# End columns of the image strips as bf16 halves read in place, four masked key copies, full-tile values, and block results copied by ScalarE

## The reference, cut to what matters

```python
# tokens: depthwise 3x3 convolution, + bias, mean over 8x8 blocks        -> 64 tokens x 128
# layer 1: attention inside an image (softmax of q k^T), residual,
#          8 experts, top 2, plus 2 shared experts (128 -> 512 -> 128, gelu)
# layer 2: 8 heads of 16 channels, rotary position on q and k;
k_c = x_c @ wk_c.T            # 15 compressed keys and values: windows of 8 tokens,
v_c = x_c @ wv_c.T            # stride 4, weighted by a softmax of 8 gate logits
win_scores  = einsum(q, k) / 4      # 64 keys, causal, window 128
comp_scores = einsum(q, k_c) / 4    # 15 compressed keys, causal
# one softmax over 64 + 15 keys and a sink; then wo, residual, and a small
# MLP over the 128 channels with lower triangular weights
```

## Time and profile before

| what | value |
|---|---|
| time, median of 3 runs | 2063.84 us (2058.97 to 2075.73) |
| the profiled execution's own time | 2071.78 us |
| its span, first to last instruction | 2070.0 us |
| busy share: PE, DVE, ACT, POOL | 84%, 61%, 46%, 46% |
| mean granted TensorE clock | 0.925 of full speed |

### The profile page before, as it was taken

One profiled execution on the slowest core, in us unless ns is written; L12 is line 12 of the kernel. 1 busy time (PEld: TensorE's weight loads), 2 busy tenths in 40 slices (PEclk: granted clock), 3 DMA queues, 4 the chain that ended last, 5 costly groups with the idle time before them and its releaser, 6 DMA issues.

```text
span 2070.0 us, 47437 instructions
## 1 busy us (share of the span) xinstructions
PE 1745.7 (84%) x15216; PEld 1352.3 (65%) x15216; DVE 1268.4 (61%) x3484; ACT 948.9 (46%) x2291; POOL 950.9 (46%) x770
## 2 busy tenths in 40 slices
PE   1454879989897989899897989899897989998956
PEld 1443766868676776768676776768675776866644
DVE  2566456757675766767575766767675756753432
ACT  0122534546463645456363635445463635553522
POOL 1224245454556555464456464464445554533222
PEclk9999988989999999999898989999998989999986
DMA  6647454544544444545445444544445444301000
GB/s 245 243 163 255 179 201 167 194 154 152 203 183 168 181 168 175 199 148 192 157 178 204 181 155 155 211 158 172 165 168 209 179 136 170 131 20 50 17 26 6
DMA packets 109170, 332.08 MB, mean 160 GB/s; under 512 B 13662, under 2 KB 87585, under 8 KB 92412
## 3 DMA queue, kind: packets, MB, share of 16 engines
q1 hardware_dynamic: 86416, 300.90, 39.5%
q0 software_dynamic: 8992, 19.42, 2.9%
q10 hardware_dynamic: 13516, 8.51, 1.4%
HBM read 299.48 MB, written 29.29 MB: 159 GB/s over the span
## 4 chain that ended last, share of the span: by engine, by line
PE 65%; POOL 10%; issue 9%; DMA 7%; DVE 4%; ACT 2%; ACTq 1%; SPq 1%; POOLq 0%; DVEq 0%
PE hid_bank L598 11%; PE pool_bank L452 6%; DMA outs_d<-ys 5%; PE pool_bank L457 5%; POOL yg L1357 5%; PE sec_bank L654 4%; PE hid_bank L583 4%; PE sec_bank L674 4%; PE hid_bank L582 3%; PE sec_bank L665 3%; POOL xbuf L1346 3%; PE hid_bank L584 2%; PE sec_bank L617 2%; PE sec_bank L634 2%; PE down_bank L543 2%
## 5 line engine op out<-in xcount | busy, mean ns | idle before, releaser
L1346 POOL TENSOR_TENSOR xbuf<-xbuf 128x512 f32<-128x512 f32 x256 | 330.1, 1289 | 528.3 <-DVE xbuf L1039 518.5
L850 ACT ACTIVATE hid<-hid_bank,bias_t 128x128 f32<-128x128 f32 x960 | 273.7, 371 | 122.3 <-PE hid_bank L584 116.4
L598 PE MATMUL hid_bank<-w_s,hid 128*128 x1920 | 291.3, 297 | 0.0
L598 PEld LDWEIGHTS hid_bank<-w_s,hid 128*128 128x128 f32 x1920 | 243.8, 199 | 16.7
L1039 DVE TENSOR_TENSOR xbuf<-xbuf 128x1536 f32<-128x1536 f32 x128 | 236.7, 1849 | 25.9 <-DMA xbuf<-in_x 25.9
L582 PE MATMUL hid_bank<-xt,w_b 128*128 128x128 bf16 x960 | 201.3, 230 | 33.8 <-issue 18.4
L1060 DVE SCALAR_TENSOR_TENSOR taps<-pooled_s,tapw,taps 128x256 f32<-128x256 f32 (+1 forms) x416 | 210.0, 505 | 29.9 <-issue 21.6
L1043 DVE TENSOR_TENSOR xbuf<-xbuf 128x512 bf16<-128x512 f32 x128 | 90.3, 706 | 213.5 <-ACT xbuf L764 213.4
L1384 POOL TENSOR_TENSOR keys_h<-keys,heads 128x632 f32<-128x632 f32 x128 | 198.6, 1578 | 18.1 <-PE sec_bank L654 15.6
L1200 DVE COPY ys<-hid_bank 128x128 f32<-128x128 f32 x240 | 68.8, 287 | 219.0 <-PE hid_bank L598 192.8
L583 PE MATMUL hid_bank<-xt,w_b 128*128 128x128 bf16 x960 | 202.9, 230 | 0.1
(11 more groups left out here) (213 smaller groups left out, 3443.7 us busy)
## 6 DMA issues: line engine op xcount, KB each, us to landing
xbuf<-in_x SPq DMA_DIRECT2D x128, 2048.0 KB
rows_s<-rows_d SPq DMA_DIRECT2D x48, 320.0 KB, 8.9
outs_d<-ys SPq DMA_DIRECT2D x240, 64.0 KB
out<-h ACTq DMA_DIRECT2D x16, 256.0 KB
w_s<-in_w ACTq DMA_DIRECT2D x1, 2560.0 KB
hid<-in_w POOLq DMA_DIRECT2D x10, 256.0 KB, 3.7
rows_d<-x2r,spot_i POOLq DMA_INDIRECT x128
yg<-outs_d,spot_i POOLq DMA_INDIRECT x128
```

The source lines that it names most:

```text
L598: mm = nc.tensor.matmul(hid_bank[n % 2][:, 0:P], hid[:, n % RING, q * P:(q + 1) * P], w_q, start=False, stop=q == FC - 1)
L850: ins = nc.scalar.activation(hid[:, n % RING, cols], hid_bank[n % 2][:, cols], ACT.Gelu, bias=bias_t[:, q, j:j + 1])
L1346: nc.gpsimd.tensor_tensor(v[:, :, 1, :], v[:, :, 1, :], v[:, :, 2 * k + 3, :], ALU.add) \
```

## The change

- **End columns.** `halves` is laid over the fp32 data itself: channel c of a column is two bf16, h = 1 its upper 16 bits and h = 0 its lower 16. A new VectorE piece `ends` takes columns 0 and 7 of a buffer in one instruction (128 x 1024 elements), subtracts the upper half from the fp32 value and writes the rest, as bf16, into the lower half. The inner sum is split the same way in column 1, so ScalarE's `inner` is gone. The end columns are then pooled by pairs of bf16 matmuls with `block_b`. All these stationary operands now lie in memory with a step of two bf16 elements, where the inner sum's was contiguous.
- **Keys.** `keys_h` holds four copies (r = 0..3) of all keys of a group; copy r keeps the channels of heads r and r+4. ScalarE makes them with a scale per partition: four `Copy` instructions of 128 x 512 (`split`) and four of 128 x 120 (`pre.5`). A score matmul takes 64 of the 128 channels (rows 0:64 or 64:128). GpSimd's eight masking instructions are gone; `roped` has a tile of its own.
- **Values.** Four fp32 matmuls with 128 token columns, two images each, and two with 128 padded compressed columns (`xc` padded to 2 x 16 for an image, cleared once). ScalarE copies them with 2 instructions of 64 x 512 and 4 of 15 x 256.
- **Block results.** `narrow`'s copy to `ys` moves from VectorE to ScalarE.
- `sb2_b` keeps one copy of the row, read four times; `before_s` shares memory; all five lists of `ORDER` are new.

```diff
 ORDER sp:
-        store.9' load.0.0 store.11' load.0.1 store.12' store.10' store.13' store.14' rows.0 rows.1 load.1.0
+        store.8' store.6' store.10' store.7' store.11' store.12' load.0.0 store.9' load.0.1 store.13' store.14'
 ORDER pe:
-        up.0 up.1 table up.2 down.0 up.3 down.1 up.4 up.5 down.2 out' up.6 down.3 down.4 pool.0.0 pool.0.1
-        pool.0.2 up.7 down.5 down.6 att.1 down.7 att.2 lift.0 pool.0.3 lift.1 widen.0 widen.1 lift.2 att.3
+        up.0 up.1 table up.2 up.3 down.0 down.1 up.4 out' up.5 down.2 up.6 up.7 down.3 down.4 down.5 pool.0.0
+        pool.0.1 down.6 pool.0.2 down.7 att.1 lift.0 lift.1 widen.0 lift.2 att.2 widen.1 att.3 lift.3 pool.0.3
...
+        pool.3.1 lift.14 narrow.11 narrow.12 widen.13 widen.14 pool.3.2 narrow.13 pool.3.3 narrow.14 post.3
 ORDER act:
-        hidden.0 table hidden.1 hidden.2 hidden.3 hidden.4 inner.0.0 hidden.5 out' hidden.6 inner.0.1 hidden.7
+        hidden.0 hidden.1 table hidden.2 hidden.3 hidden.4 out' hidden.5 hidden.6 hidden.7 lift.0 att.1 lift.1
 ORDER dve:
-        tap.1.8' pair.0.0 tap.1.9' tap.1.10' tap.1.11' tap.1.12' tap.1.13' tap.1.14' inner.0.0 pair.0.1 att.0
+        tap.1.10' tap.1.11' tap.1.12' tap.1.13' tap.1.14' pair.0.0 ends.0.0 pair.0.1 att.0 inner.0.0 ends.0.1
 ORDER pool:
-        scatter.7' gather.0 gather.1 gather.2 gather.3 add.0.0 gather.4 add.0.1 gather.5 gather.6 gather.7
-        add.0.2 add.0.3 att.0 pre.1 add.1.0 add.1.1 pre.3 pre.4 pre.6 add.1.2 add.1.3 pre.7 score.2 score.4
+        scatter.6' scatter.7' gather.0 gather.1 gather.2 gather.3 gather.4 gather.5 gather.6 add.0.0 gather.7
+        add.0.1 add.0.2 att.0 add.0.3 pre.1 add.1.0 add.1.1 pre.3 pre.4 add.1.2 add.1.3 add.2.0 add.2.1 add.2.2
...
-        halves = [b[:].bitcast(bf16).rearrange("p (b x) (h c) -> p b x h c", x=8, h=2) for b in xbuf]
+        halves = [b[:].bitcast(bf16).rearrange("p (b x) (c h) -> p b x h c", x=8, h=2) for b in xbuf]
...
 PE, pool:
                     if k in (0, 2):
-                        eng.wait_ge(x_in[v], at(x_in[v], g, 16 * (u + 1)))
+                        eng.wait_ge(ends_low, at(ends_low, g, 2 * u + v + 1))
...
-                                nc.tensor.matmul(view[:, 0, :, side[bx]], halves[v][:, bx, 4, h, :], block_b[:],
+                                nc.tensor.matmul(view[:, 0, :, side[bx]], halves[v][:, bx, 1, h, :], block_b[:],
                                                  start=h == 0, stop=h == 1)
                         for bx in range(BX // 2):
-                            mm = nc.tensor.matmul(view[:, 1, :, side[bx]], blocks[v][:, bx, 0, :], block_sum[:],
-                                                  start=True, stop=True)
+                            for h in range(2):
+                                mm = nc.tensor.matmul(view[:, 1, :, side[bx]], halves[v][:, bx, 0, h, :], block_b[:],
+                                                      start=h == 0, stop=h == 1)
...
 PE, values:
-                    for m in range(4):
-                        im = 4 * half + m
-                        nc.tensor.matmul(bank[0:L, m * C:(m + 1) * C], x3t[:, im * L:(im + 1) * L], second["v"][:],
-                                         start=True, stop=True)
-                        mm = nc.tensor.matmul(bank[L:LK, m * C:(m + 1) * C], xc[:, im, :], second["vc"][:],
-                                              start=True, stop=True)
+                        for t in range(T):
+                            mm = nc.tensor.matmul(b1[:, t * C:(t + 1) * C], x3t[:, t * P:(t + 1) * P], second["v"][:],
+                                                  start=True, stop=True)
...
+                        for k in range(2):
+                            mm = nc.tensor.matmul(b0[:, k * C:(k + 1) * C],
+                                                  xc[:, 4 * k:4 * k + 4, :].rearrange("p i w -> p (i w)"), second["vc"][:],
+                                                  start=True, stop=True)
 PE, score:
-                            q3[:, tok:tok + L], keys_h[:, t % 2, im, half * HH:(half + 1) * HH, :],
+                            q3[rows, tok:tok + L], keys_h[rows, :, 2 * t + im, :],
...
 ACT:
-                if kind == "inner":
-                    eng.wait_ge(x_summed, at(x_summed, g, 4 * u + 2 * k + 2))
-                    nc.scalar.activation(halves[k][:, :, 4, 0, :], blocks[k][:, :, 1, :], ACT.Copy) \
-                      .then_inc(inner_high, 1)
+                elif kind == "narrow":
+                    k = j % SLOTS
+                    eng.wait_ge(hid_used, at(hid_used, g, NS * FC + j + 1))
+                    if j >= SLOTS:
+                        eng.wait_ge(stored[k], at(stored[k], g, 16 * (j // SLOTS)))
...
+                    nc.scalar.activation(ys[:, k, :], hid_bank[(NS * FC + j) % 2][:, 0:P], ACT.Copy).then_inc(out_ready, 1)
...
+                elif kind == "split":
+                    eng.wait_ge(rope_added, at(rope_added, g, 2))
...
+                    for r in range(HH):
+                        ins = nc.scalar.activation(keys_h[:, r, :, 0:L], keys, ACT.Copy, scale=heads[:, r:r + 1])
+                    ins.then_inc(keys_ready, 1)
 DVE:
                 elif kind == "inner":
-                    eng.wait_ge(inner_high, at(inner_high, g, 2 * u + k + 1))
-                    nc.vector.tensor_tensor(halves[k][:, :, 4, 1, :], blocks[k][:, :, 1, :], halves[k][:, :, 4, 0, :],
+                    eng.wait_ge(x_summed, at(x_summed, g, 4 * u + 2 * k + 2))
+                    nc.vector.tensor_tensor(halves[k][:, :, 1, 0, :], blocks[k][:, :, 1, :], halves[k][:, :, 1, 1, :],
                                             ALU.subtract).then_inc(inner_low, 1)
+                elif kind == "ends":
+                    eng.wait_ge(x_in[k], at(x_in[k], g, 16 * (u + 1)))
+                    nc.vector.tensor_tensor(halves[k][:, :, 0:8:7, 0, :], blocks[k][:, :, 0:8:7, :],
+                                            halves[k][:, :, 0:8:7, 1, :], ALU.subtract).then_inc(ends_low, 1)
...
-                    nc.vector.tensor_copy(ys[:, k, :], hid_bank[(NS * FC + j) % 2][:, 0:P]).then_inc(out_ready, 1)
```

More of the change, by code:

```diff
@@ L35 @@
 LK = L + LC
+LCP = 16
 HH = HEADS // 2
@@ L46 @@
 STAGES = ("tok", "att", "ffn", "sec")
-STAGE_OF = dict(pair="tok", add="tok", inner="tok", pool="tok", tap="tok", out="tok",
+STAGE_OF = dict(pair="tok", add="tok", inner="tok", ends="tok", pool="tok", tap="tok", out="tok",
                 att="att", low="att", high="att", rest="att", scatter="att", up="ffn", hidden="ffn", down="ffn", moe="ffn",
@@ L50 @@
                 gate="ffn", load="tok", keep="set", gather="sec", mix="sec", pre="sec",
-                score="sec", exp="sec", turn="sec", value="sec", post="sec", weights="set")
+                score="sec", exp="sec", turn="sec", value="sec", post="sec", split="sec", weights="set")
 ORDER = dict(
     sp="""
-        store.9' load.0.0 store.11' load.0.1 store.12' store.10' store.13' store.14' rows.0 rows.1 load.1.0
-        load.1.1 load.2.0 store.0 store.3 load.2.1 store.1 rows.2 store.5 load.3.0 store.2 load.3.1 store.4
@@ new lines @@
+        lift.13 widen.12 narrow.11 lift.14 narrow.12 widen.13 pool.3.2 widen.14 pool.3.3 narrow.13 narrow.14
+        post.3 post.4 post.5 weights.0 weights.1 weights.2 weights.3 weights.4 weights.5 weights.6 weights.7
+        weights.8 weights.9""",
+    dve="""
+        tap.1.10' tap.1.11' tap.1.12' tap.1.13' tap.1.14' pair.0.0 ends.0.0 pair.0.1 att.0 inner.0.0 ends.0.1
+        att.1 moe mix pre.1 inner.0.1 pre.2 pair.1.0 ends.1.0 att.4 pre.3 att.5 inner.1.0 pre.4 pre.5 pair.1.1
+        att.7 ends.1.1 gate inner.1.1 score.0 score.1 pair.2.0 score.2 score.3 tap.0.0 score.4 score.5 inner.2.0
+        score.6 score.7 ends.2.0 tap.0.1 att.8 tap.0.2 pair.2.1 tap.0.3 att.9 ends.2.1 value.0 inner.2.1 att.10
+        tap.0.4 value.1 pair.3.0 tap.0.5 value.2 tap.0.6 ends.3.0 value.3 att.11 inner.3.0 value.4 pair.3.1 rest
+        value.5 ends.3.1 value.6 tap.0.7 tap.0.8 value.7 tap.0.9 att.12 tap.0.10 post.1 tap.0.11 post.2 tap.0.12
+        inner.3.1 tap.0.13 low post.3 tap.0.14 tap.1.0 tap.1.1 tap.1.2 tap.1.3 tap.1.4 tap.1.5 tap.1.6 tap.1.7
+        tap.1.8 post.5 tap.1.9 weights.0 weights.1 weights.2 weights.3 weights.4 weights.5 weights.6 weights.7
+        weights.8 weights.9""",
@@ L170, in program @@
         b1_s = sb("b1_s", [P, NS * FC])
-        sb2_b = sb("sb2_b", [P, T, C], bf16)
+        sb2_b = sb("sb2_b", [P, C], bf16)
         second = {}
@@ L456, in tokens @@
                         for bx in range(BX // 2):
-                            mm = nc.tensor.matmul(view[:, :, v, side[bx]], blocks[v][:, bx, 7, :], block_sum[:],
-                                                  start=True, stop=True)
+                            for h in range(2):
+                                mm = nc.tensor.matmul(view[:, :, v, side[bx]], halves[v][:, bx, 7, h, :], block_b[:],
+                                                      start=h == 0, stop=h == 1)
```

157 lines of the change are left out of this document (72 added, 85 removed).

## The result

Slower: 2247.05 us (median of 4 runs, 2240.44 to 2267.01) against 2069.78 (4 runs) for the kernel before on the same chip, a ratio of 1.088 with a 95% interval of 1.079 to 1.097. The forecast was 1870. The profiled execution took 2241.62 us.

The account below looks back on a forecast made before the run. PE's matmuls set the pace: 116.7 - 12.6 - 4.1 = 100.0 us an iteration, plus 3 for DVE. Thirteen iterations x 13.7 = 178, plus 8 and 12, took 198 off 2071.8: 1874, so about 1870 us; 8-in-10 range 1815 to 1975.

Parts of the forecast that it names:

- PE, end columns: End-column pooling on PE: eight strided bf16 matmuls take 0.20 us at full clock, saving 12.6 us an iteration.
- Rival 3: Pooling on PE: strided weights load as slowly as fp32 records, 0.865 us for eight; about 2090 us, chance 0.08 in full.
- saved 12.6 us: End columns on PE: matmul time an iteration falls from 16.4 to 3.8 us.
- 100.0 us account: PE's time for one iteration: 116.7 - 12.6 - 4.1 = 100.0 us.
- PE, values: Value matmuls: eight pairs, 5.4 us, become six full-width matmuls, 1.34 us; saved 4.1 us an iteration.
- PE, scores: Score matmuls with half the rows: bounds -2.7 to +2.3 us an iteration, taken as 0.
- The start of the iteration: Around `pool.0.0`: it starts 3.0 us later, 3.1 us of work moves ahead of the pause; the two cancel.
- 0, or +3 if the cover is gone: `store.9` behind a 2 MB load, `narrow.14`'s copy waiting 2 to 3 us, with PE's pause as cover.
- DVE: VectorE's load rises from 77.7 to 83.6 us an iteration; 3 us added to the iteration, making 103 us.
- Rival 1: VectorE takes over: iteration 107 to 110 us, about 1955 us; chance 0.30 together with rival 2 and halfway rival 3.
- Rival 2: ScalarE's `narrow` copies each 0.3 to 0.5 us late: about 1950 us; chance 0.30 with rival 1 and halfway rival 3.
- PE's waits name ScalarE's ys copy: Sign in the profile that would show the forecast wrong by ScalarE as a tollgate, about 1950 us.

Follow-up runs that it names:

- b_ends_free: Kernel before with end columns and inner sums as bf16 halves read in place, no `ends`, lower halves of columns 0 and 7 left out: 2001.48 us, 0.967.
- b_vals: Kernel before with the full-tile values alone (four plus two matmuls, padded compressed columns, ScalarE's six copies): 2150.64 us, ratio 1.038.
- sp_stores: Changed kernel with only SyncE's list reordered, stores only behind loads whose buffer TensorE has already read: 2124.84 us, ratio 1.024 against the kernel before.
- b_ends_23: Kernel before with inner sums read in place, and `ends` and halved end columns only for tiles u = 2 and 3 of four: ratio 1.034.
- b_fill: Kernel before with 22 more matmuls of 512 columns before `up.6`, their result overwritten: 2116.39 us, ratio 1.021.

## Why the prediction was wrong, and where it was right

*PE, end columns: size right, use wrong.* Strided weights are as fast as contiguous ones here: the chain's "0.21 PE pool_bank L463 x8" is my 0.20. This agrees with what the Trainium skill (TensorE: Matmul & The Clock Gate, section on weight-path perf modes) says of weights that are "packed or strided". Rival 3, my other side, had nothing to it. But "saved 12.6 us" was taken as 12.6 us of iteration. On the order before, the cheaper matmuls brought 36 us in the run; on the new order the whole pooling part brings 135, `ends` and the sums in place included. TensorE then waits for others (before `widen` for VectorE's `ys` copy 38.2 us in b_ends_free, which has no `ends`, and 11.6 in the kernel before), and a wait may be followed by more at half clock. That the matmuls left alone would keep their pace was a term of the 100.0 us account that I never wrote down: the pooling's and the values' groups did fall, from 366.8 to 159.5 and from 105.4 to 33.3 us, but all others together rose by 13%, from 1977 to 2228 us (sums over groups, whose records overlap, so they exceed the busy time of the engine).

*PE, values: the same.* The six took 1.5 us (b_vals), near my 1.34, and alone the edit costs 79 us, partly through the pause shown above, partly unsettled.

*PE, scores: held.* At full clock two matmuls take 0.69 us at 64 rows against 0.68; the mean of 637 ns in the group above mixes full and half clock (shortest 426, median 727; 455 in the mean before). The Trainium skill (TensorEngine Tiling (Array Packing), section on the theoretical speedup) has up to twice the speed for a dimension of at most 64; no run here shows that.

*The start of the iteration: the failing step.* I saw `store.9` behind a load, priced it "0, or +3 if the cover is gone", and did not carry the same reading to the rest of SyncE's list, where `store.1`, `store.2` and `store.5` stand behind `load.3.0` and `load.3.1`. The price was in my own: 7.16 us for a store behind a load. The list costs 122 us, shown by sp_stores. `store.9` itself I had at nothing, with PE's pause as cover, and there was no cover: it landed after 9.05 us, `narrow.14` waited 5.52 us for it, and the x3t copy stood behind; TensorE's wait before L696 rose from 6.9 to 58.8 us, 3.2 an iteration, which is the "+3" that I wrote and did not take. That the same list would have cost less with the copy still on VectorE, where no p3t or x3t copy stands behind it, is likely and not shown: no run has the one without the other.

*DVE: the load right, the place missing.* I said 83.6 us an iteration; it is 87.3. The 3.7 are in the main `ends` at 1561 ns (2.3 us more) and the inner split at 899, which the earlier trace rows has at 706 (1.5). I set contention at nought by a sum of GpSimd's busy time. The trace says otherwise:

```profile
1391.56 2.78 POOL L1371 TENSOR_TENSOR xbuf<-xbuf 128x512 f32<-128x512 f32 x2 [17.24 <-DVE xbuf L1067]
1394.44 2.04 POOL L1343 TENSOR_TENSOR rs<-ve,power 128x4 f32<-128x4 f32 x1
```

```profile
1393.11 1.25 DVE L1052 TENSOR_TENSOR ve<-ve,mv 128x4 f32<-128x4 f32 x1
1394.29 1.35 DVE L1075 TENSOR_TENSOR xbuf<-xbuf 128x1024 bf16<-128x1024 f32 x1
```

VectorE's 1393.11 adds four columns and takes 0.16 us in the median; beside GpSimd's adds it takes 1.25, until they end. GpSimd's power of four columns takes 2.04 beside the `ends` of 1394.29. Its median was 1.03 us in the kernel before. By the rule that I quoted (the Trainium skill, SBUF — State Buffer, section on the two separate sides) one of the two waits until the other has ended, and these rows agree. My error was to apply it to totals: what counts is which two instructions stand beside each other.

*Rivals.* Rival 1, VectorE as the bound: VectorE is 65 to 71% busy in full iterations, so it is no bound, but its order is one (b_ends_23). The sum of this rival was off as well: 23.9 and 81 to 85 us are 105 to 109, not 107 to 110. Rival 2, ScalarE as a tollgate: right in kind and it was my sign "PE's waits name ScalarE's ys copy"; I gave 1950 us for it since I counted each copy 0.3 to 0.5 us late and not the ones that stand 3.6 to 5.5 us behind a store. ScalarE's load, 61.7 us an iteration, was forecast well (62.6) and told nothing. GpSimd's is 51.3, where 58.1 - 12.6 = 45.5 was the forecast: its adds are longer by 3.2 us an iteration and its power instructions by 1.8.

*The whole.* The forecast was a gain of about 200 us and the run lost 2247 - 2070 = 177: 122 are the stores' order (shown). The other 50 to 55 are a balance of parts whose worth depends on the order: in the new order the pooling is worth 135 us and holds `ends` at 37; in the old one the pooling, the values and the copies each cost something alone, 81, 79 and 61 us by their ratios. The masked keys were not tried alone, and what each part is worth inside this balance stays open.

## What to carry to other kernels

Microseconds taken from a busy engine are not microseconds of the iteration: ask, for each, which wait then ends last, and allow for half clock behind a new pause (13.6 us of it followed one of 2.23 us here). When a copy moves to another engine, walk the whole list of what its waits depend on, here every store that stands behind a load, and what stands behind the copy in its new list. Try the parts alone: one of them, reading the high halves in place with no new instruction, was worth 1.6% by itself.

## What the chip showed that was not expected

- Soon after a pause of 2.23 us TensorE passed 13.6 us at a granted clock of 0.51 with 13.0 us busy (b_vals); after one of 1.51 us, with 22 filler matmuls ahead of it, the clock fell as well, to 0.56 in the mean of 7 us (b_fill).
- A 64 KB store issued right behind a 2 MB load landed after 7.00 us, another after 9.05; with the list of sp_stores the median of all stores is 1.5, against 3.1.
- A VectorE instruction on 128x4 elements took 1.25 us in place of 0.16 beside GpSimd's add, and GpSimd's add, 1.53 us at most in the kernel before, up to 3.94 in the changed one.
